# Scores from q and k cut into two float32r parts on 64 rows, even and odd heads on the two halves of the array

## The reference, cut to what matters

```python
q, k, v = proj(wq, bq), proj(wk, bk), proj(wv, bv)           # 16 heads of 16
scores = jnp.einsum('bhqd,bhkd->bhqk', q, k) / np.sqrt(16)
attn = softmax(scores + rel_bias[bucket(k_pos - q_pos)])     # all 1024 keys, no causal mask
out = jnp.einsum('bhqk,bhkd->bhqd', attn, v)
```

## Time and profile before

| | before |
|---|---|
| median of 3 runs | 3385.61 us (3383.04 to 3396.36) |
| the profiled execution, its span | 3385.0 us |
| PE busy with matmuls | 3038.8 us, 90% |
| DVE busy | 2054.3 us, 61% |
| ACT busy | 1713.4 us, 51% |
| POOL busy | 1304.5 us, 39% |
| one batch | 416 us |

### The profile page before, as it was taken

How to read it: one execution, slowest core, us unless ns; L and a number is a source line. 1 busy time by engine, 2 the same in 40 slices (tenths; PEclk the granted TensorE clock), 3 DMA queues, 4 the chain that set the end, 5 groups by cost and what they waited for, 6 DMA issues and landing times.

```text
span 3385.0 us, 51303 instructions
## 1 busy us (share of the span) xinstructions
PE 3038.8 (90%) x14692; PEld 1389.2 (41%) x14692; DVE 2054.3 (61%) x3333; ACT 1713.4 (51%) x3668; POOL 1304.5 (39%) x1816
## 2 busy tenths in 40 slices
PE   6979999799997999879998799988999789997898
PEld 4623266223661236512365133652346523464224
DVE  4568645686456854478544785447854478544784
ACT  2427733377343763337633476334763347533575
POOL 2324533244332443424434244342443334433344
PEclk8979999799997999979999799997999979998899
DMA  5050000500004000140001300023000320003200
GB/s 147 13 112 1 2 14 13 112 2 1 14 24 101 1 1 14 42 83 1 1 14 51 75 1 1 14 58 68 2 7 8 68 58 1 8 8 74 51 1 13
DMA packets 71931, 108.66 MB, mean 32 GB/s; under 512 B 10896, under 2 KB 33472, under 8 KB 71488
## 3 DMA queue, kind: packets, MB, share of 16 engines
q1 hardware_dynamic: 71616, 104.91, 13.3%
HBM read 70.07 MB, written 36.72 MB: 32 GB/s over the span
## 4 chain that ended last, share of the span: by engine, by line
PE 64%; issue 8%; DVE 8%; DMA 7%; ACT 5%; POOL 4%; SPq 2%; ACTq 0%; DVEq 0%; POOLq 0%
PE psum L629 13%; PE psum L607 13%; PE psum L578 12%; PE psum L478 10%; PE psum L682 3%; DVE mx L1248 3%; DMA SQ<-mrow 2%; DMA SK<-parts 2%; ACT Z L999 2%; PE psum L663 2%; PE psum L723 2%; PE psum L497 2%; DMA parts<-Z 2%; POOL X L1338 2%; PE psum L709 2%
## 5 line engine op out<-in xcount | busy, mean ns | idle before, releaser
L1248 DVE TENSOR_REDUCE mx<-psum 128x1 f32<-128x1024 f32 x1024 | 1205.1, 1219 | 411.0 <-PE psum L578 411.0
L999 ACT ACTIVATE Z<-psum 128x512 f32<-128x512 f32 x2048 | 1103.5, 598 | 482.0 <-PE psum L607 479.7
L1426 POOL TENSOR_TENSOR Z<-Z,band_exp 128x256 f32<-128x256 f32 (+1 forms) x1152 | 713.0, 640 | 1040.2 <-ACT Z L999 1029.4
L578 PE MATMUL psum<-SK,SQ 96*128 96x512 bf16 x2048 | 626.2, 426 | 117.6 <-DMA SK<-parts 94.1
L607 PE MATMUL psum<-SQ,SK 128*128 128x512 bf16 x2048 | 647.7, 389 | 93.5 <-DMA SQ<-mrow 67.6
L629 PE MATMUL psum<-Z,Vx 128*17 128x512 f32 x4096 | 538.3, 599 | 4.2
L607 PEld LDWEIGHTS psum<-SQ,SK 128*128 128x128 bf16 x2048 | 165.4, 97 | 725.5 <-ACT Z L999 581.3
L478 PE MATMUL psum<-Wqkvg,Z 128*128 128x512 f32 x768 | 374.5, 614 | 25.0 <-ACT Z L906 22.5
L578 PEld LDWEIGHTS psum<-SK,SQ 96*128 96x128 bf16 x2048 | 189.7, 101 | 476.1 <-DVE mx L1248 179.3
L1368 POOL TENSOR_TENSOR Z<-Z 128x512 f32<-128x512 f32 x64 | 81.2, 1269 | 313.2 <-DVE Z L1177 313.2
L478 PEld LDWEIGHTS psum<-Wqkvg,Z 128*128 128x128 f32 x768 | 137.4, 191 | 153.5 <-issue 150.5
(11 more groups left out here) (124 smaller groups left out, 3363.6 us busy)
## 6 DMA issues: line engine op xcount, KB each, us to landing
parts<-Z SPq DMA_DIRECT2D x96, 256.0 KB
Xin<-L_attn_a_x SPq DMA_DIRECT2D x9, 1024.0 KB, 5.6
out<-X SPq DMA_DIRECT2D x16, 512.0 KB, 3.2
SQ<-parts SPq DMA_DIRECT2D x16, 384.0 KB, 6.4
SQ<-parts SPq DMA_DIRECT2D x24, 256.0 KB, 9.1
SK<-parts SPq DMA_DIRECT2D x16, 384.0 KB, 8.2
SK<-parts SPq DMA_DIRECT2D x24, 256.0 KB, 11.8
SQ<-parts SPq DMA_DIRECT2D x8, 768.0 KB, 8.8
```

The lines of the kernel that those rows point to most:

```text
L578: mm = pe.matmul(bank[2 * (u % 2) + k], SQ[0:MAX_ROW, h, i * P:i * P + P], SK[0:MAX_ROW, h, 512 * k:512 * k + 512], start=True, stop=True)
L999: nc.scalar.activation(ring[:, n % RING, :], col_bank(s, c), ACT.Exp)\
L1248: nc.vector.tensor_reduce(mx[:, blk, col:col + 1], bank_pair[u % 2], AX_X, ALU.max)\
L1426: nc.gpsimd.tensor_tensor(ring[:, n % RING, a:z], ring[:, n % RING, a:z], band_exp[:, 4 * hg + c, at:at + z - a], ALU.mult)\
```

## The change

q and k are cut into two float32r parts instead of three bf16 parts (float32r: four bytes, rounded as the matmul reads them). Three products are kept, on 3 x 16 = 48 rows; with 14 bias rows, one that is free for the row maximum (row 63) and one more the stack has 64 rows. Even heads lie on partitions 0 to 63, odd heads on 64 to 127. The middle part (DVE, L1243) and POOL's low part (L1403) fall away; the second part is the remainder that DVE L1239 writes. The stores are 8 of 512 KB, the spreads 24 (two runs of rows, two halves). PE's order in a step becomes: R C0 R C1, W, R C2 R C3, where the two matmuls of a neighbouring R and C lie on different halves; C0 and C1 are heads 1 and 3 of the four, C2 and C3 heads 0 and 2.

```diff
-PARTS = 3
-Q_PARTS = (2, 1, 0, 1, 0, 0)
-K_PARTS = (0, 1, 2, 0, 1, 0)
-RUNS = ((0, 3), (3, 2), (5, 1))
-MAX_ROW = 96
+PARTS = 2
+HALF = 64
+RUNS = ((0, 0, 2), (32, 1, 1))
+FIXED = 32
+BIAS_ROW = 48
+MAX_ROW = 63
+COLS = (1, 3, 0, 2)
...
-        SQ = sb("SQ", [P, HEADS, T], BF16)
-        SK = sb("SK", [P, HEADS, T], BF16)
+        SQ = sb("SQ", [P, HEADS // 2, T], F32R)
+        SK = sb("SK", [P, HEADS // 2, T], F32R)
...
+        def rows_of(h, n=HALF):
+            return slice(HALF * (h % 2), HALF * (h % 2) + n)
...
                 for part in range(PARTS):
-                    slot = (PARTS - 1 - part, part)[s]
+                    slot = (1 - part, part)[s]
                     sp.dma_start(parts_scratch[s, 8 * h:8 * h + 8, slot],
-                                 cmp[:, h, s, part, :]).then_inc(parts_out[s].sem, 16)
+                                 split[h][s][:, part, :].bitcast(F32)).then_inc(parts_out[s].sem, 16)
...
+                for row, q_slot, length in RUNS:
+                    slot = (q_slot, 0)[s]
+                    for half in range(2):
+                        r0 = HALF * half + row
+                        sp.dma_start(stack[r0:r0 + HD * length, heads.start // 2:heads.stop // 2, :],
+                                     parts_scratch[s, heads.start + half:heads.stop:2, slot:slot + length]
+                                     .rearrange("h k d n -> (k d) h n")).then_inc(spread[share].sem, 16)
...
-                for k in range(2):
-                    mm = pe.matmul(bank[2 * (u % 2) + k], SQ[0:MAX_ROW, h, i * P:i * P + P],
-                                   SK[0:MAX_ROW, h, 512 * k:512 * k + 512], start=True, stop=True)
-                mm.then_inc(mx_s.sem, 1)
+                mm = pe.matmul(bank[2 * (u % 2) + k], SQ[rows_of(h, MAX_ROW), h // 2, i * P:i * P + P],
+                               SK[rows_of(h, MAX_ROW), h // 2, 512 * k:512 * k + 512], start=True, stop=True)
...
+                    u = AHEAD + 2 * s
                     if s < NS:
-                        for c in range(4):
-                            score_cols(b, s, c)
-                            while c == 1 and u < units[s]:
-                                score_rows(b, u)
-                                u += 1
+                        for k in range(2):
+                            if u < NU:
+                                score_rows(b, u, k)
+                            score_cols(b, s, k)
...
                     if s >= LAG:
                         weigh(b, s - LAG)
+                    if s < NS:
+                        for k in range(2):
+                            if u + 1 < NU:
+                                score_rows(b, u + 1, k)
+                            score_cols(b, s, 2 + k)
+                        if block_before(s) is not None:
+                            max_transpose(b, block_before(s))
...
-                    need(dve, c_r1, b, n + 1)
-                    nc.vector.tensor_copy(cmp[:, h, s, 1, tok], r1[:, n % 2, :]).then_inc(c_mid.sem, 1)
...
-                for n in range(8):
-                    h, g, s = qk_order(n)
-                    need(pool, c_mid, b, n + 1)
-                    tok = slice(512 * g, 512 * g + 512)
-                    nc.gpsimd.tensor_tensor(cmp[:, h, s, 2, tok], r1[:, n % 2, :], cmp[:, h, s, 1, tok],
-                                            ALU.subtract).then_inc(c_lo.sem, 1)
```

More of the change, by code:

```diff
@@ L16 @@
 F32 = mybir.dt.float32
-BF16 = mybir.dt.bfloat16
+F32R = mybir.dt.float32r
 ALU = mybir.AluOpType
@@ L255, in build @@
         c_hi = tally("act", "c_hi", 8)
[L256 to L260, removed]
+        c_lo = tally("dve", "c_lo", 8)
+        parts_out = [tally("sp", f"parts_out_{side}", 4, 16) for side in "qk"]
+        spread = [tally("sp", f"spread{share}", 8, 16) for share in range(3)]
         p_vx = tally("pe", "p_vx", 4)
@@ L389, in parts_store @@
                 for part in range(PARTS):
-                    slot = (PARTS - 1 - part, part)[s]
+                    slot = (1 - part, part)[s]
                     sp.dma_start(parts_scratch[s, 8 * h:8 * h + 8, slot],
-                                 cmp[:, h, s, part, :]).then_inc(parts_out[s].sem, 16)
+                                 split[h][s][:, part, :].bitcast(F32)).then_inc(parts_out[s].sem, 16)
             def spread_rows(b, share, s):
                 heads = SHARES[share]
[L397 to L403, removed]
+                need(sp, parts_out[s], b, 2 * (heads.start // 8) + 2)
+                stack = (SQ_words, SK_words)[s]
+                for row, q_slot, length in RUNS:
+                    slot = (q_slot, 0)[s]
+                    for half in range(2):
+                        r0 = HALF * half + row
+                        sp.dma_start(stack[r0:r0 + HD * length, heads.start // 2:heads.stop // 2, :],
+                                     parts_scratch[s, heads.start + half:heads.stop:2, slot:slot + length]
+                                     .rearrange("h k d n -> (k d) h n")).then_inc(spread[share].sem, 16)
             with sp.Fori(0, B) as b:
@@ L599, in score_cols @@
                     need(pe, vx_cp, b, 4)
-                elif s == WIDE.start and c >= 2:
+                elif s == WIDE.start and i >= 2:
                     need(pe, mx_r, b, NU)
@@ L1456, in shape_constants @@
     bucket = np.where(n < 16, n, np.minimum(big, BUCKETS - 1))
-    rows = np.zeros((32, 64))
-    rows[0, 0:8] = 1
-    for part in range(PARTS):
-        for j in range(8):
-            r, blk = 1 + 8 * part + j, np.arange(8)
-            rows[r, 0:8] = blk == j
-            rows[r, 8:16] = blk < j
-            rows[r, 16:24] = blk > j + 1
-            rows[r, 24], rows[r, 25] = -(part >= 1), -(part >= 2)
+    rows = np.zeros((P, 64))
+    blk = np.arange(8)
+    for first in (0, HALF):
+        rows[first + MAX_ROW, 0:8] = 1
+        for part in range(PARTS):
+            for j in range(1, 8):
+                r = first + BIAS_ROW + 7 * part + j - 1
+                rows[r, 0:8] = blk == j
+                rows[r, 8:16] = blk < j
+                rows[r, 16:24] = (blk > j + 1) * 1.0 - (blk > 1)
+                rows[r, 24] = -part
     return {
```

132 lines of the change are left out of this document (68 added, 64 removed).

## The result

The changed kernel takes 3666.02 us (median of 4 runs, 3660.86 to 3673.68); the kernel before, run beside it, 3388.29 us (3383.04 to 3396.36). The ratio is 1.0813, 95% interval 1.0790 to 1.0836: 8% slower. The forecast was 3459 us, 2.2% slower, with a range up to 3530. The direction was right; the loss is 278 us instead of 74.

The account below looks back on a forecast made before the run. The loop was taken to be bound by a ring of latencies, 2.87 us a step, not by PE's work. Terms +5.1 + 6.5 - 3.4 + 1.0 = +9.2 us per batch, x 8 = +74, gave 3459 us; range 3340 to 3530.

Parts of the forecast that it names:

- the ring: Main loop: matmul delays, two exponentials and W in series make each step 2.87 us, before and after the change.
- the output transposes: Head of a loop step: seven transposes per batch become covered by PE's wait for a bank, -3.4 us per batch.
- R ahead of C2: Loop, after W: R delays C2 by a weight load, 0.10 us in 51 steps, +5.1 us per batch (0 to +11.0).
- PE is the bound: Main loop: halved score matmuls shorten steps down to DVE's 2.35 us, 28 us per batch, 3165 us; chance 5%.
- The output copy: One loop step in eight: W, now straight after C1, waits for ACT's copy; six per batch, +6.5 us.
- rival 4: Main loop: PE's clock stays at 1.2 GHz, steps take 4.2 us, +66 us per batch, 3990 us; chance 5%.
- From cutting to the loop: Path ahead of the loop: shorter cutting against more store bytes, -1.7 to +3.7 us, taken as +1.0 per batch.
- the shorter cutting: Ahead of the stores: DVE's middle part and POOL's low part leave the path, -1.7 us per batch with hand-overs.
- The spreads carry the same bytes: Spreads ahead of the loop: same bytes in 24 DMAs for 18; extra issues pass while DMA engines are full.
- The first 22 units keep DVE's pace: Units ahead of the loop: DVE still sets their pace, so no time is added.
- Rival 2: Spreads: DMAs to both halves run side by side near 389 GB/s, -4.8 us per batch, 3347 us; chance 12%.
- Rival 3: R and C matmuls: float32r costs two passes (about 3690 us) or four (over 4400 us); chance 9%.

Follow-up runs that it names:

- Order and halves in bf16: The changed kernel with bf16 wherever it has float32r, same order, halves and 24 spreads, less exact scores: 3276.98 us, ratio 0.9671.
- the early copy: The changed kernel with ACT's output copy half a step earlier, behind the last exponential of the step before: 3546.37 us, ratio 1.0460.
- bf16 in sequence: The kernel before with only PE's new order, its bf16 96-row stacks kept, so R and C cannot overlap: 3493.61 us, ratio 1.0305.
- Without overlap in float32r: The changed kernel with the order of heads turned, so each R and the C behind it lie on one half: 4086.11 us, ratio 1.2037.

## Why the prediction was wrong in size, point by point

The direction and the ring were right. Three terms of the sum failed: the front (+1.0, measured +10.0), the output transposes (-3.4, measured +4.5) and R ahead of C2 (+5.1, measured +10.7).

**The ring: right.** Halving the scores' time on PE made no ordinary step shorter. Order and halves in bf16 give 2.87, the value before; the rival "PE is the bound" is out.

**"R ahead of C2", +5.1 forecast, 51 x 0.21 = +10.7 measured: mis-sized, and for another reason.** The forecast put a weight load between R and C2. There is none: the loads of the two halves run side by side. The delay lies in float32r's own first matmul after a wait (record 0.50 for 0.39), and the ring passes two of them, not one. That bf16 in the same order has it not is shown; that the longer weight load is the cause (0.18 for 0.10) is argued from the two numbers, and from the records of 0.39 where the load is done ahead.

**The output copy, +6.5: right.** 6 x ((4.33 - 3.08) - (3.03 - 2.87)) = +6.5.

**The output transposes, -3.4 forecast, +4.5 measured: this step failed, and with it rival 4.** With the halves they are covered where the clock is full (3.10 with the early copy). But the forecast let PE stand idle for the copy and priced that wait at its length only. The clock falls to 1.2 GHz behind it, the transposes' step becomes 4.31 in the mean, and the term is 6 x ((4.31 - 3.08) - (3.35 - 2.87)) = +4.5 (for six; the seventh lies in the loop's last steps). Rival 4 asked whether the clock would stay low through the loop; it did not see that it could fall inside it, six times a batch. At the loop's start rival 4 was right in small: the first step between two W takes 4.32 instead of 2.94 us, +1.4, at a clock of 0.50 to 0.60 for 1.00. Why the same wait of 1.16 us takes the clock down 45 times in 48 with float32r pairs, 8 times with bf16 pairs and never with bf16 in sequence stays open; the runs show that the idle wait is needed for it.

**From cutting to the loop, +1.0 forecast, +10.0 measured: the largest error.** The -1.7 for the shorter cutting was right: the first store goes out 6.1 us after the front's start instead of 7.8. The rest failed. The 1.05 MB of stores cost +3.3 alone (2.4 by the medians), out of 0 to +5.4 in the forecast. "The spreads carry the same bytes" was priced at nothing, with only the issue of six more DMAs looked at; cutting runs of 48 rows into 32 and 16 costs +6.1. Both together are +10.5 in the profile and +8.9 by the medians; less the 1.7 that is +7.2 to +8.8 of the +10.0, and 1.2 to 2.8 us are not assigned. "The first 22 units keep DVE's pace" failed too (27.9 us for 25.1); how much of its 2.8 us lies hidden under the spreads of share 2 was not tested. Nor was it told apart whether the smaller reach of a DMA or a cost of each DMA makes the +6.1. The forecast also put the 9.15 us of the row maxima down to their place in SP's queue; from ACT's queue they took 9.28. The Trainium skill (SBUF — State Buffer, Door 1: The DMA port swizzle) would have 32 rows below 64 reach half of the ports; the forecast's estimate from it, 16 units of time for 14, has the right sign and was set aside. But it spreads 48 rows evenly over the ports that they reach. By the same section's map rows 32 to 47 lie on the ports of rows 0 to 15, which gives, as an estimate, 16 units before and after, and no reason for the +6.1. No run here shows the ports.

**Rival 2: refuted.** DMAs to both halves in turn do not go faster: 187 and 177 GB/s in the two stages after, 178 and 195 before. Rival 3: refuted as well, one pass.

**What is not assigned.** In the loop the terms above give 10.7 + 6.5 + 4.5 + 1.4 - 0.2 (the first step's share of the 51) = +22.9 of +26.0. That is also what the first 50 steps between two W lost in sum, with two smaller differences that cancel: +0.8 in steps behind a low clock, and -0.7 since `max_transpose`, 0.11 in each of six steps before, has left the ring. The other +3.1 lies in the last 13, where four banks are free and the output of the last group follows; nothing was tested there.

**The sum again, with measured terms:** +10.0 - 1.9 + 26.0 + 0.4 = +34.4 per batch (of unrounded terms), 275 us.

## What to carry to other kernels

Before pricing a faster matmul, close the ring of waits: if one step is exponentials, a delay and a fixed matmul, the saved array time only becomes idle time, and each new idle stretch is to be priced twice, by its length and by what the clock may do to the step behind it. Where an engine ahead of a ring waits for a helper's copy, put the copy half a step earlier: one line gave back 120 us here. A DMA cut into narrower pieces of the same bytes is not free when the engines are loaded, and small DMAs issued behind it paid for it on either of the two queues tried.

## What the runs showed of the hardware

- float32r streamed 512 columns in 0.23 to 0.25 us in a row, one pass. A matmul that starts after a wait took 0.50 us to its result, 0.11 more than bf16; one whose weights were loaded ahead took 0.39.
- Two matmuls on rows 0 to 63 and 64 to 127 start within 0.01 us of each other, weight loads too. On one half they start 0.24 to 0.34 us apart (step 3.31 for 3.08).
- Behind a wait of 1.2 us PE's granted clock fell to half in 45 of 48 cases in the float32r kernel, in 8 of 48 with bf16 on the two halves, in none with bf16 in sequence, and in none with five unread matmuls in the wait. Without overlap in float32r it was 0.81 over the loop shown.
- The same 6.3 MB per batch in 24 DMAs of 32 and 16 rows instead of 18 of 48, 32 and 16 came 6.1 us later in the profile, 5.9 by the medians of the runs.
